# A transformer block on one core: both pairs of heads in one load of keys, rows and zeros; first loads and stores waited for in another order; two products ahead of the first projection

## What is computed

```python
Q, K, V = x @ qw, x @ kw, x @ vw          # 16 heads of 8
Q, K = rope(Q, freq), rope(K, freq)
score = einsum('bhqd,bhkd->bhqk', Q, K) / sqrt(8) - 1e10 * (1 - causal)
weights = softmax(score - max(score))
x = layernorm(x + merged(weights @ V) @ ow)
gates = top2 of softmax(x @ router_w + router_b), renormalised, over 4 experts
h = silu(x @ w1[e]) * (x @ w3[e]);  out = sum_e gates[e] * (h @ w2[e])
x = layernorm(x + out)
```

## Time and profile before

| | before |
|---|---|
| median of 3 executions | 426.69 us (424.84 to 427.38) |
| profiled execution | 426.87 us, its span 425.2 us |
| start to first product (PE L1121) | 7.06 us |
| first score product (PE L1163) | 25.39 us |
| first transposed product of the first stage that waits for rows | 69.16 us |
| steady stages | 25.8 to 25.9 us each |
| PE busy, share of the span | 91% |

### The profile page before, as it was taken

One profiled execution on the slowest core, in us unless ns is written; L12 is line 12 of the kernel. 1 busy time (PEld: TensorE's weight loads), 2 busy tenths in 40 slices (PEclk: granted clock), 3 DMA queues, 4 the chain that ended last, 5 costly groups with the idle time before them and its releaser, 6 DMA issues.

```text
span 425.2 us, 7512 instructions
## 1 busy us (share of the span) xinstructions
PE 386.5 (91%) x2398; PEld 204.4 (48%) x2420; DVE 318.7 (75%) x1034; ACT 262.9 (62%) x373; POOL 189.7 (45%) x254
## 2 busy tenths in 40 slices
PE   3758578999999999999999999999999999999992
PEld 1344122232322323323232333788888888888781
DVE  2859888989999999999999964346567558656744
ACT  1232523777786776868768687665766656575560
POOL 7135621143351524426134242366456646655662
PEclk9979695999999999999999999999999999999998
DMA  7465651041312213132220000000000000000000
GB/s 223 151 194 102 233 169 27 16 101 25 95 26 69 54 32 87 21 80 50 58 53 4 0 3 0 2 2 1 0 2 25 1 2 21 6 1 3 25 0 25
DMA packets 45260, 21.13 MB, mean 50 GB/s; under 512 B 31011, under 2 KB 42915, under 8 KB 45222
## 3 DMA queue, kind: packets, MB, share of 16 engines
q1 hardware_dynamic: 44406, 19.81, 17.9%
q10 hardware_dynamic: 816, 0.85, 0.8%
HBM read 13.11 MB, written 7.35 MB: 48 GB/s over the span
## 4 chain that ended last, share of the span: by engine, by line
PE 73%; DVE 10%; DMA 4%; issue 3%; POOL 3%; ACT 3%; SPq 3%; ACTq 0%; POOLq 0%; DVEq 0%
PE o_bank L1206 13%; PE bank L1280 10%; PE t_bank L1280 10%; PE t_bank L1293 10%; PE bank L1163 9%; PE t_bank L1188 8%; PE small_bank L1163 4%; DMA q_op<-max_rows 3%; SPq L453 3%; DVE mg_t L900 2%; DVE mg_w L900 2%; PE o_bank L1302 2%; POOL roped L521 1%; DVE x_w L900 1%; PE t_bank L1121 1%
## 5 line engine op out<-in xcount | busy, mean ns | idle before, releaser
L718 ACT ACTIVATE num<-t_bank 128x1024 f32<-128x1024 f32 (+2 forms) x160 | 142.5, 939 | 59.8 <-PE t_bank L1188 59.0
L624 POOL TENSOR_TENSOR hid_lo<-num,q_op 128x512 fp32r<-128x512 f32 x63 | 81.8, 1301 | 57.8 <-ACT q_op L774 56.6
L586 POOL TENSOR_SCALAR_AFFINE_SELECT num<-num 128x512 f32<-128x512 f32 x64 | 40.0, 636 | 116.6 <-ACT num L718 116.5
L1206 PE MATMUL o_bank<-num,v_op 128*32 128x512 f32 (+3 forms) x768 | 80.1, 497 | 0.3 <-DVE maxima L900 0.3
L1163 PE MATMUL bank<-k_op,q_op 128*128 128x512 bf16 (+7 forms) x243 | 67.0, 331 | 9.3 <-DMA k_op<-k_scratch 3.6
L774 ACT ACTIVATE q_op<-num 128x512 fp32r<-128x512 f32 x64 | 40.5, 632 | 42.7 <-DVE num L1053 42.1
L904 DVE TENSOR_REDUCE maxima<-bank 128x1 f32<-128x512 f32 x83 | 55.3, 685 | 3.4 <-PE bank L1163 2.1
L1188 PE MATMUL t_bank<-q_op,k_op 64*128 64x512 bf16 (+3 forms) x384 | 50.0, 336 | 7.0 <-DMA q_op<-max_rows 2.9
L1163 PEld LDWEIGHTS bank<-k_op,q_op 128*128 128x128 bf16 x257 | 21.2, 99 | 59.9 <-DVE maxima L904 22.5
L1053 DVE TENSOR_TENSOR num<-bank,num 128x512 f32<-128x512 f32 x32 | 22.1, 692 | 34.3 <-ACT num L781 33.6
L900 DVE CUSTOM_DVE_ANT_0 mg_w<-bank,resid 128x256 f32<-128x256 f32 (+7 forms) x94 | 39.5, 440 | 4.6 <-PE bank L1163 3.9
(11 more groups left out here) (151 smaller groups left out, 630.5 us busy)
## 6 DMA issues: line engine op xcount, KB each, us to landing
q_op<-q_scratch SPq DMA_DIRECT2D x64, 48.0 KB
w_raw<-in_w_all SPq DMA_DIRECT2D x6, 512.0 KB, 4.1
k_op<-k_scratch SPq DMA_DIRECT2D x60, 48.0 KB, 1.9
xT<-in_x_feat SPq DMA_DIRECT2D x4, 256.0 KB, 6.2
q_op<-max_rows SPq DMA_DIRECT2D x64, 3.0 KB
q_scratch<-num SPq DMA_DIRECT2D x2, 384.0 KB, 3.0
k_scratch<-num SPq DMA_DIRECT2D x2, 384.0 KB, 2.8
q_scratch<-x_res SPq DMA_DIRECT2D x2, 384.0 KB, 3.2
```

What stands on the lines that cost most here:

```text
L586: pool.affine_select(out=tile, in_=tile, compare_op=ALU.is_ge, fill=0.0, base=0, pattern=[[0, GH], [1, P]], channel_multiplier=-1)\
L624: pool.tensor_tensor(hid_lo[:, m % HB, :], hid[:, m % HB, :], hid_hi[:, m % HB, :].bitcast(F32), ALU.subtract).then_inc(f_lo, 1)
L718: act.activation(num[:, t % PB, :, off:CH].rearrange("p (k i) t -> p i k t", i=2)[:, :, h:h + each, :], t_bank[k % TB][:, :, 0:each * (CH ...
L1206: ins = pe.matmul(o_bank[h * QD:(h + 1) * QD, off:CH], v_op[w][:, kt, h, :], num[:, t % PB, h, off:CH], start=kt == 0, stop=kt == TI * (c ...
```

## The change

Six edits, of which none changes what is computed:

1. `load_k` sends both pairs of heads in one DMA: two DMAs of 48x2x512 in place of four of 48x512.
2. `q_op` is laid out by half, pair and block, and `max_part` by part and pair, so that the rows of the maxima of both pairs go in one DMA: `send_rows` issues two DMAs of 3x16x64 in place of four of 3x8x64. The zeros go in two DMAs in place of four.
3. `parts_stored` is split by queries and keys; `load_q` for the first group waits for the queries' stores only.
4. The weights of queries and keys are issued by ACT ahead of the tables; SP begins with the first chunk of x. ACT's and SP's credits (`sem_inc`) come after these DMAs.
5. DVE's `memset` of `causal` is its first instruction.
6. PE waits for that `memset` and runs two float32 products of 128 by 448 columns on it, whose result in `o_bank` nobody reads, ahead of its wait for `rot_ready`.

```diff
-        q_op = [... .rearrange("p (r j i q) -> p r j i q", r=NPR, i=2, q=QB) for flat in q_flat]
+        q_op = [... .rearrange("p (c k i q) -> p c k i q", c=NC, i=2, q=QB) for flat in q_flat]
-        parts_stored = [sem(f"parts_stored{i}") for i in range(CHUNKS)]
+        parts_stored = [[sem(f"parts_stored{i}{x}") for x in "qk"] for i in range(CHUNKS)]
...
-                if n > 1:
-                    eng.dma_start(q_op[u][i * HR + KROWS:i * HR + QROWS, pr, c * NB:(c + 1) * NB, i, :],
-                                  z_dram[:, c * CH:(c + 1) * CH]).then_inc(q_loaded[u][c], 16)
+                if n > 1 and pr == 0:
+                    eng.dma_start(q_op[u][i * HR + KROWS:i * HR + QROWS, c, :, i, :], z_dram)\
+                        .then_inc(q_loaded[u][c], 16)
         def load_k(eng, n, u, c):
-            for h in range(GH):
-                pr, i = divmod(h, 2)
-                at = (n * GH + h) * DH
-                eng.dma_start(k_op[u][i * HR:i * HR + KROWS, pr, c * CH:(c + 1) * CH],
-                              k_dram[at:at + DH, :, c * CH:(c + 1) * CH].rearrange("d r t -> (d r) t"))\
-                    .then_inc(k_loaded[u][c], 16)
+            cols = slice(c * CH, (c + 1) * CH)
+            by_pair = k_dram[n * GH * DH:(n + 1) * GH * DH, :, cols].rearrange("(p i d) r t -> i (d r) p t", p=NPR, i=2)
+            for i in range(2):
+                eng.dma_start(k_op[u][i * HR:i * HR + KROWS, :, cols], by_pair[i, :, :, :]).then_inc(k_loaded[u][c], 16)
...
-            sp.sem_inc(out_stored, 16)
-            for w, i in ((qw, 0), (kw, 2)):
-                sp.dma_start(wqk[:, i, :], w).then_inc(ld_proj, 16)
             for ch in range(CHUNKS):
                 sp.dma_start(xT[:, ch * CH:(ch + 1) * CH], x_feat[:, ch * CH:(ch + 1) * CH]).then_inc(ld_x[ch], 16)
...
-            sp.wait_ge(parts_stored[0], 2 * PARTS * 16)
-            load_q(sp, 0, 0, 0, range(GH))
+            sp.wait_ge(parts_stored[0][0], PARTS * 16)
+            load_q(sp, 0, 0, 0)
...
-                for h in range(GH):
-                    sp.dma_start(
-                        q_op[to][h % 2 * HR + KROWS:h % 2 * HR + QROWS, h // 2, c * NB:(c + 1) * NB, h % 2, :],
-                        max_rows[c][h // 2 * PARTS * NB:(h // 2 + 1) * PARTS * NB, h % 2 * QB:(h % 2 + 1) * QB])\
+                for i in range(2):
+                    sp.dma_start(q_op[to][i * HR + KROWS:i * HR + QROWS, c, :, i, :],
+                                 max_rows[c][:, i * QB:(i + 1) * QB])\
                         .then_inc(rows_loaded[c], 16)
...
         def _(act):
+            for w, i in ((qw, 0), (kw, 2)):
+                act.dma_start(wqk[:, i, :], w).then_inc(ld_proj, 16)
+            load_table(act, 0)
             for credit in (c_hi, c_mgs, c_store, o_copied):
                 act.sem_inc(credit, 1)
-            load_table(act, 0)
...
         def _(dve):
+            dve.memset(causal[:, 0:CH - QB], 0.0).then_inc(causal_cleared, 1)
...
         def _(pe):
+            pe.wait_ge(causal_cleared, 1)
+            for _ in range(WARM):
+                pe.matmul(o_bank[:, 0:CH - QB], causal[:, 0:P], causal[:, 0:CH - QB], start=True, stop=True)
```

More of the change, by code:

```diff
@@ L296, in transformer_block @@
         q_flat = [sb(f"q_op{u}", [P, NPR * S], F32R) for u in range(2)]
-        q_op = [flat[:, :].bitcast(BF16).rearrange("p (r j i q) -> p r j i q", r=NPR, i=2, q=QB) for flat in q_flat]
+        q_op = [flat[:, :].bitcast(BF16).rearrange("p (c k i q) -> p c k i q", c=NC, i=2, q=QB) for flat in q_flat]
         k_flat = [sb(f"k_op{u}", [P, NPR * S // 2], F32R) for u in range(2)]
@@ L314, in transformer_block @@
         neg_max, rest = sb("neg_max", [P, NPR, NB]), sb("rest", [P, NPR, NB])
-        max_part = [sb(f"max_part{c}", [P, NPR, PARTS, NB], BF16) for c in range(NC)]
+        max_part = [sb(f"max_part{c}", [P, PARTS, NPR, NB], BF16) for c in range(NC)]
         max_rows = [sb(f"max_rows{c}", [NPR * PARTS * NB, P], BF16) for c in range(NC)]
@@ L381, in load_table, with load_q @@
             eng.dma_start(sin_sb[:, cols], sin_t[:, cols]).then_inc(ld_tab[c], 16)
[L383 to L394 removed]
+        def load_q(eng, n, u, c):
             for h in range(GH):
@@ L420, in _ @@
             sp.wait_ge(ops_filled, 1)
-            sp.dma_start(z_dram, q_op[0][0:PARTS, 0, 0:NB, :, :].rearrange("p j i q -> p (j i q)"))\
+            sp.dma_start(z_dram, q_op[0][0:PARTS, 0, 0:NB, :, :].rearrange("p k i q -> p (k i q)"))\
                 .then_inc(zeros_stored, 16)
@@ L445, in _ @@
             for c in range(NC):
-                load_q(sp, 1, 1, c, range(GH))
+                sp.wait_ge(parts_stored[c][1], PARTS * 16)
+                load_q(sp, 1, 1, c)
                 load_k(sp, 1, 1, c)
@@ L461, in _ @@
             for ch in range(NC, CHUNKS):
-                sp.wait_ge(parts_stored[ch], 2 * PARTS * 16)
+                for stored in parts_stored[ch]:
+                    sp.wait_ge(stored, PARTS * 16)
             sp.wait_ge(zeros_stored, 16)
@@ L480, in stage @@
                         sp.wait_ge(t_ready, NT * n + SEG_T[0])
-                        load_q(sp, s + 1, v, 0, range(GH))
+                        load_q(sp, s + 1, v, 0)
                     if step == ("T", 1, TI, 0, 0):
@@ L488, in stage @@
                         sp.wait_ge(t_ready, NT * n + NT)
-                        load_q(sp, s + 1, v, 1, range(GH))
+                        load_q(sp, s + 1, v, 1)
                         load_k(sp, s + 1, v, 1)
@@ L549, in split_max @@
                 then(pool.tensor_scalar(neg_max[:, :, :], top, -1.0, None, ALU.mult), 1)
-                then(pool.tensor_copy(part[:, :, 0, :], neg_max[:, :, :]), 2)
-                then(pool.tensor_tensor(rest[:, :, :], neg_max[:, :, :], part[:, :, 0, :], ALU.subtract), 3)
-                then(pool.tensor_copy(part[:, :, 1, :], rest[:, :, :]), 4)
-                then(pool.tensor_tensor(part[:, :, 2, :], rest[:, :, :], part[:, :, 1, :], ALU.subtract), 5)
+                then(pool.tensor_copy(part[:, 0, :, :], neg_max[:, :, :]), 2)
+                then(pool.tensor_tensor(rest[:, :, :], neg_max[:, :, :], part[:, 0, :, :], ALU.subtract), 3)
+                then(pool.tensor_copy(part[:, 1, :, :], rest[:, :, :]), 4)
+                then(pool.tensor_tensor(part[:, 2, :, :], rest[:, :, :], part[:, 1, :, :], ALU.subtract), 5)
                 pool.sem_inc(max_split, 1)
@@ L696, in _ @@
             for ch in range(NC):
-                act.wait_ge(parts_stored[ch], 2 * PARTS * 16)
+                for stored in parts_stored[ch]:
+                    act.wait_ge(stored, PARTS * 16)
             act.sem_inc(t_exped, TB)
@@ L830, in _ @@
             dve.sem_inc(f_lo, HB)
-            dve.memset(causal[:, 0:CH - QB], 0.0).then_inc(causal_cleared, 1)
             for u in range(2):
@@ L1157, in stage @@
                         _, c, prs, j, half = step
-                        once(q_loaded[u][c], (2 * turn_u - 1) * (16 * GH), ("q", c))
-                        once(k_loaded[u][half], turn_u * (16 * GH), ("k", half))
+                        once(q_loaded[u][c], (16 * GH) + (turn_u - 1) * (16 * (GH + 2)), ("q", c))
+                        once(k_loaded[u][half], turn_u * (16 * 2), ("k", half))
                         lo, width = half * CH, s_width(j, half)
@@ L1180, in stage @@
                         off, heads = t_off(c, kt), t_heads(c, kt)
-                        once(rows_loaded[c], (n + ahead + 1) * (16 * GH), ("m", c, ahead))
+                        once(rows_loaded[c], (n + ahead + 1) * (16 * 2), ("m", c, ahead))
                         pe.wait_ge(t_exped, k + 1)
@@ L1190, in stage @@
                                                 k_op[w][rows, pr, kt * P:(kt + 1) * P],
-                                                q_op[w][rows, pr, c * NB + off // QB:(c + 1) * NB, i, :],
+                                                q_op[w][rows, c, pr * NB + off // QB:(pr + 1) * NB, i, :],
                                                 start=True, stop=True, tile_position=(i * HR, 0))
```

25 lines of the change are left out of this document (13 added, 12 removed).

## The result

| | before | changed |
|---|---|---|
| median, same chip, 11 executions each | 425.78 us | 423.18 us |
| ratio | | 0.994 (0.9919 to 0.996) |
| span of the profiled execution | 425.2 us | 421.2 us |
| start to first projection | 7.06 us | 6.84 us |
| waits for the rows of the maxima | seven, 2.9 us | none |

One of the changed kernel's 11 executions took 540.51 us at a mean granted clock of 0.65, against 0.965 to 0.972 in the others; the median includes it, the ratio leaves it out.

A forecast was written before the change was run, and what follows sets the result against it. PE, busy for 91% of the span, was taken as the bound, with waits in start, prologue and stages. 1.71 + 0.12 + 0.63 + 0.60 = 3.06 us off 426.87 gave 423.8 profiled, 423.6 median; range 420.8 to 426.0.

The forecast's parts named there:

- Start, 1.71: Kernel start: with weights and x issued earlier, PE's first projection begins at 5.35 in place of 7.06, gaining 1.71 us.
- Added products, nothing: Kernel start: two added products before PE's first projection cost nothing and, given the pause after them, are counted as no gain.
- rival B: Kernel start: added products raise the clock early, 1.6 us more gain, 422.0 us; chance 0.31.
- Keys' loads, 0.12: Prologue: fewer key-load issues on ACT bring its second part sooner, 0.15 us at most, 0.12 taken.
- Rows: Stages: two doubled sends land in 2.5 to 3.2 us, removing PE's waits; 0.63 in the first stage, 0.60 in steady ones.
- The steady term: Six steady stages: PE's 0.38 wait goes, but only DVE's 0.10 of idle time is won each, 0.60 us in all.
- The first stage was put at 0.63: First stage: DVE itself waited for PE, so removing the wait for rows counts in full, 0.63 us.
- I count no change: Prologue and first stage: low clock stretches follow PE's idle time, which keeps its pattern, so no gain or loss.
- C: Start and sends: x lands as late as before, start gain 0.95, sends gain nothing, 425.6 us; chance 0.13.
- A: Whole kernel: the summed gains of start, prologue and stages hold, 423.6 us; chance 0.42.
- D, slower: Stages: doubled sends land 0.97 us later, seven times, 6.8 us lost, 431.7 us; chance 0.07.
- E: Low clock stretches: earlier work closes idle time ahead of one, so the clock gains more, 420.5 us or below; chance 0.07.

The follow-up runs named there:

- the start alone: The kernel before with only the first loads reordered, the memset first and two added products: 425.9 us, ratio 0.9993 (0.997 to 1.0015).
- the keys' loads alone: The kernel before with only the keys' loads in two DMAs and the queries' and keys' stores waited for apart: 425.11 us, ratio 0.9989 (0.9976 to 1.0003).

## Why the prediction was right in its number, and where not

- **Start, 1.71: wrong.** The step that failed is the landing of the weights: "On ACT they are again a second DMA, issued at about 1.3, so again 4.5." They landed at 6.05. A landing time was carried over from a row where other loads were in flight. PE gained 0.22, which is within what its start varies by; the start alone gave 0.3 us (interval 1.3 to a loss of 0.6). Below it, x too had been put 1.6 us too early (5.59 in place of 4.0), by the row of a load that had landed in 3.1.
- **Added products, nothing: between.** No row had shown a rise after a pause, and two products don't bring it reliably. What rival B described (its first four records at half the duration) happened with three products, and was followed by its own named limit, the sine table. Where B was given 1.6 us, the step from two products to three was worth 0.7 us by the ratios, with intervals that overlap.
- **Keys' loads, 0.12: right in mechanism.** ACT's second part came right behind DVE, and the values' projection 0.16 earlier, 0.11 of it by the edit. The time (0.5, interval 1.0 to none) doesn't contradict it.
- **Rows: right in mechanism, its size somewhat small.** Issue 0.71 (range 0.70 to 1.05), no wait left, DVE next in line, stages of 25.65 (25.7 to 25.8 forecast). The steady term was 6 × 0.10 and measured 6 × 0.15: the wait took more from the stage than DVE's idle time right behind it. The first stage was put at 0.63 and the ruler moves by 1.6 there. This is the last low stretch of the changed kernel; it held 9.9 us in the earlier trace rows:

```profile
61.00:67.70 6.70, 5.55 (x17) 1.95 (x16) 6.25 (x28) 0.41 (x1) 0.68 (x4) 0.50 0.12 18
```

So "I count no change" for these stretches was a mis-sized term, but its cause is only half settled. Of the four kernels with four sends, three have 10 us there and the one with the keys' loads alone 3.3 (its windows below); of the ten with two sends, six have 6.7 and four 3.3.

```profile
63.80:67.10 3.30, 3.28 (x10) 1.34 (x10) 2.95 (x14) 0.00 (x0) 0.00 (x0) 0.50 0.02 3
```

The time from the copy at 62 to that at 76 follows this length: 14.82 to 15.21 us in the three kernels with 10 us, 13.62 to 13.79 with 6.7, 13.27 to 13.30 in the four with 3.3 and two sends. How much of the 0.63 the sends account for by themselves isn't settled. In the one kernel with four sends and a low stretch of 3.3, the first stage has a wait of 0.52 and takes 13.47, only some 0.2 more than the four without a wait. Among the three with 10 us, the stage takes 15.21 with a wait of 0.63 and 14.82 with one of 0.19, so there nearly all of it counts. PE's idle time ahead of the rise may have a part in the length of the stretch, since only kernels with four sends have the long one, and so has chance.

Nor are the low stretches of this pair shorter as a whole. The first one of the changed kernel is longer than the 6.80 us of the earlier trace rows:

```profile
20.00:30.20 10.20, 6.60 (x26) 4.04 (x25) 5.65 (x24) 3.69 (x7) 3.62 (x4) 0.50 0.77 212
```

From edge to edge the three stretches hold 6.8, 6.8 and 10.2 us in the kernel before and 10.2, 6.8 and 6.8 in the changed one, 23.8 in both; the repeated changed kernel has 17.1. So the 4.0 between the profiled pair has chance in it in the prologue and in the first stage, and the gain to go by is the 2.6 of the medians.

- **The sum.** 1.4 us too much for the start, 0.4 too little for the rows and 0.35 too little for the loads; the last two lie within the noise of their runs. The number came near by luck: errors of both signs stood in it, and the median that it was taken from was 0.9 too high. The start ended below even C's 0.95, though its interval holds that, and the rows above A's 1.23. The 1% that the prediction took for what a measurement tells from no change was too much as well: some ten executions each told 0.6% from none.
- **D, slower, fell.** A send of twice the size is no later than before: had it been 0.97 later, waits would be in the trace, and there are none. **E** came only in part: the last low stretch is shorter, the first one longer.

## What to carry to other kernels

A landing time belongs to the loads in flight around it, not to the DMA: where a first load is moved, take every row of that size as a bound, and expect small loads beside a large one to be later, by up to 3 us here. Issues of small DMAs on one queue are worth merging where something waits for the last of them; but price the gain by the engine that is late next, and test that engine by giving it more work. Whether work added to keep the clock up has done so shows in the durations of the very next products; here it was sure only with the longer run that ended about 1 us or less ahead of them. And before a difference of two profiles is given a cause, profile the same kernel twice: here that alone moved the end of the prologue by 1.6 us.

## What was not expected of the hardware

- The issue of a send took 0.70 us at 3x8x64 and 0.71 at 3x16x64, but that of the zeros doubled with its size. The row of the kernel before (issue in ns, min/median/max), and that of the changed one:

```profile
L391 SPq DMA_DIRECT2D q_op<-zeros x48: 341/350/353, 68.5 to 217.6; - x48
```

```profile
L392 SPq DMA_DIRECT2D q_op<-zeros x24: 705/711/729, 64.7 to 212.4; - x24
```

Sends and zeros have the same destination, size and queue; they differ by their source (24, then 48 partitions of SBUF; DRAM). So merging saved issue time for the sends and none for the zeros.
- 64 KB landed 1.9 to 2.1 us after issue when each was first on its queue and no 256 KB had been issued by then; with 256 KB issued at the same instant as the first of two on one queue, the two took 3.2 to 4.0 and 4.7 to 5.1 in all kernels with such a start.
- Of 0.43 us more on DVE, 0.27 reached the end of a stage, though DVE is idle there for 1.55 us: the idle time of DVE, which hands over to PE at every step, was room for less than half of the added work.
- Where records are missing from a trace, idle time is overstated: PE's idle time in the same steady stage reads 0.64 us in a trace with 199 records of it and 0.18 in one with 202, for periods of the same length.
